# Cross-attention and a routed mixture of experts: the first five shared-expert steps run inside attention's last five, with the last tiles' routing behind them

## The chip, the cores and the metric

One core of one Trainium2 chip. The metric is the device time of one execution in microseconds (us), the slowest core's; here there is only one. Engines: TensorE (PE) multiplies matrices, VectorE (DVE), ScalarE (ACT) and GpSimd (POOL) work elementwise, SyncE (SP) issues DMAs. Each takes its instructions in the order of its own list and waits on semaphores.

## The reference

x is 4096 rows of 256 (4 batches of 1024), the context 4 x 64 rows of 192. Cut to what matters:

```python
x = x + attention(layernorm(x), ctx, Wq, Wk, Wv, Wo, bo)      # 16 heads of 64, 64 keys
xf = layernorm(x)                                              # rows for the experts
scores = softmax(xf @ gate_w.T); idx = top_k(scores + gate_b, 2)
expert(x) = silu((x @ w1 + b1) * (x @ w3 + b3)) @ w2 + b2      # 256 -> 352 -> 256
out = x + sum of the two chosen experts, weighted by their scores (8 experts) + shared expert
```

## The kernel before

The 4096 rows are 32 tiles of 128 (NT = 32). Weights are split into a high part in a rounded format and a low part, the rest; each product is three matmuls (high by high, high by low, low by high). The kernel has three stages.

**Preparation** (up to about 100 us) folds Wq with the keys and Wo with the values.

**Attention** is a software pipeline of steps s (lines 329 to 1407). In step s each engine works on several tiles: on TensorE (`tile_step`, L1329) scores of tile s-1, gate product of s-6 (L1360), transposes of the probabilities of s-3 (L1376), output product of s-4, and the transposes of the normalized xn2 of s-5 (L1404). These and the gate product share PSUM bank 0, so the transposes of tile t wait until the gate logits of t-1 are copied (`lg_ok`, L1398). On VectorE: maxima, sums, the low part pTl, x2 (L1083) with its statistics, and the logits copy (L1030). On GpSimd: reciprocal roots of the variance (L610 to L614, L605 on) and the scaling of the probabilities. On ScalarE: exponentials, xn2 (L766), pTh (L783) and xn2T (L759). Steps 33 to 37 have no scores left: the pipeline runs empty. In them ScalarE and VectorE also begin to split the experts' weights (`high13`, L882; `low13`, L1150). `begin_step` of each engine is what it does in a step besides `tile_step`.

**Routing** is done in groups of eight tiles. The three first groups (GROUPS) are routed in six small stages (`route`, L975) in steps of attention; the last eight tiles (REST) after it (`rest`, L1216). The routed rows are put in order by expert: GpSimd scatters a record of each row and choice to a table in DRAM (`scatter_record`, L665, three in flight, 64 in all, one tile of two per step from step 20 on), SyncE then loads 71 slices of it (L543), and GpSimd gathers the rows (`gather`, L714).

**Shared and routed steps** (`unit_step` of each engine: L906, L1164, L1409) are one pipeline over 103 tiles: 20 shared ones, 71 routed ones, 12 shared. In step s: the input of tile s is split (uxTh on ScalarE, L939; uxTl on VectorE, L1177), TensorE multiplies tile s-1 by w1 and w3 ("UV", 12 matmuls of 352 columns, L1464), VectorE adds the bias and multiplies (uv L1195, hid L1198), ScalarE applies SiLU to tile s-2 (L949), TensorE transposes hid of s-3 (L1456), ScalarE and VectorE split that (hTh L944, hTl L1182), and TensorE makes the output product of s-4 (L1440). The first twenty steps also carry the splitting of the other weights (`high2`, `low2`, `high13`, `low13`).

The order is written by hand for each engine. VectorE's, between attention and the common loop, is the one that the change rewrites: rest(0), step 0, rest(1), rest(2), step 1, rest(3), rest(4), step 2, rest(5), step 3, unit arithmetic, step 4, more unit arithmetic (L1221 to L1256). Tiles, DRAM scratch and buffers share SBUF over time: a region is given to later buffers when the work that used it is over, which the waits on `O_ok`, `lg_ok` and the DMA semaphores guard.

Of the kernel before, what the change touches and what calls it, by code (L numbers as in the profile page):

```python
# [13 lines left out]
P = 128  # L14
# [12 lines left out]
def xattn_moe(nc, x, ctx, Wq, Wk, Wv, Wo, bo, gate_w, gate_b, w1, b1, w3, b3, w2, b2,  # L27
# [23 lines left out]
    RING = 8  # L51
# [28 lines left out]
    with stack:  # L80
# [67 lines left out]

        xin = sb("xin", [P, 2, D], F32, att)
# [7 lines left out]

        pre = ExitStack()
        raw = ExitStack()
        wv_raw = sb("wv_raw", [P, 2, INNER], F32, raw)  # L160
        wo_raw = sb("wo_raw", [P, NJ, D], F32, raw)
        raw.close()
        wvl = sb("wvl", [P, 2, INNER], F32R, pre)
# [6 lines left out]

        xres = sb("xres", [P, 2, D], F32, att)
        xn2T = sb("xn2T", [P, 2, D], F32, att)
# [3 lines left out]
        x2 = sb("x2", [P, 2, D], F32, att)  # L176
        xn2 = sb("xn2", [P, 2, D], F32, att)
# [14 lines left out]
        gv = sb("gv", [P, 6, 8], F32, att)  # L192
# [32 lines left out]
        b13 = sb("b13", [P, E, 2 * H], F32)  # L225
# [6 lines left out]
        uv = sb("uv", [P, 2, H], F32)  # L232
        logits = sb("logits", [P, NT, E], F32)
# [7 lines left out]
        unit_no = sb("unit_no", [P, NU], F32)  # L241

# [142 lines left out]
        FILL = 5  # L385
        
# [59 lines left out]
        def _(sp):  # L446
# [51 lines left out]
            def load_w13(e):  # L498
                sp.wait_ge(O_ok, TPB if e < EARLY13 else 2 * TPB)
                sp.dma_start(w13_raw[:, e, :, 0:H], w1[e, :, :].rearrange("(k p) h -> p k h", p=P)).then_inc(raw13_in[e], 16)  # L500
                sp.dma_start(w13_raw[:, e, :, H:2 * H], w3[e, :, :].rearrange("(k p) h -> p k h", p=P)).then_inc(raw13_in[e], 16)
# [7 lines left out]
            def begin_step(s, par):  # L509
                tile_step(s, par)  # L510
                if s in (13, 14, 15, 16, 17):
                    load_w13(s - 13)
                if s in (21, 22, 23):
                    load_w13(s - 16)
                if 24 <= s < 24 + EARLY2:
                    load_w2(s - 24)
                if s in (31, 32):
                    load_w2(s - 25)
                if 24 <= s < 24 + RING:
                    for half in xn2T_out:  # L520
                        sp.wait_ge(half, 16 * RING // 2)
                    shared_x(s - 24)
# [22 lines left out]
            for t in range(RING, NA):  # L545
                shared_x(t)
# [30 lines left out]
        def _(pool):  # L577
# [93 lines left out]
            def begin_step(s, par):  # L671
# [22 lines left out]


            for half in xn2_out + x2_out:
                pool.wait_ge(half, before(NT))
            pool.wait_ge(O_ok, NT)
            pool.wait_ge(lg_ok, NT)
            pool.memset(hid[:, :, H:H3], 0.0).then_inc(hid_one, 1)  # L700
            pool.wait_ge(hid_one, 1)
            pool.memset(hid[:, :, H:H + 1], 1.0).then_inc(hid_one, 1)
# [24 lines left out]

            ahead = RING - 2
# [15 lines left out]
        def _(act):  # L744
# [118 lines left out]
            def begin_step(s, par):  # L863
# [4 lines left out]
                tile_step(s, par)  # L868
                if 33 <= s < 33 + EARLY13:
# [26 lines left out]
            act.wait_ge(zero_ok, 1)  # L896
            steps(NT, 1, 6, begin_step, begun=0)

            act.wait_ge(rt_sub, len(GROUPS) + 1)
            act.activation(rest_score[:, :, :], rest_marked[:, 0, :, :], ACT.Exp).then_inc(rt_exp, 1)  # L900

# [4 lines left out]
            def unit_step(s, m, routed=None):  # L906
# [4 lines left out]
                if has(t, NALL):  # L911
# [10 lines left out]
                    elif t < R0:  # L922
                        wait(act, Y_ok, t + 1)
                        wait(act, shared_row_out[y], 16 * (t // YRING))
# [32 lines left out]
            act.wait_ge(hid_one, 2)  # L957
            act.wait_ge(zero_out, 16 * (NB // QUAD + 3))
            unit_steps(act, unit_step)
# [3 lines left out]
        def _(dve):  # L963
# [196 lines left out]

            dve.wait_ge(small_in, 80)
            steps(NT, 2, 6, begin_step, begun=0)

            def unit_step(s, m, routed=None):  # L1164
# [19 lines left out]
                if has(t, NALL):  # L1184
                    p = (m + 1) % 2
                    if is_routed(t, routed):
                        e = dve.value_load(expert_of[0:1, bass.ds(t - R0, 1)], min_val=0, max_val=E - 1)
                        if isinstance(t, int) and t == R0:
                            dve.wait_ge(b13_in, 32 * E)
                        bias = b13[:, bass.ds(e, 1), :].rearrange("p e (a h) -> p (e a) h", a=2)  # L1190
# [20 lines left out]

            dve.wait_ge(lg_ok, NT)
# [32 lines left out]
            unit_step(4, 4)  # L1245
# [258 lines left out]
```

## Time and profile before

| | us |
|---|---|
| median of 3 runs | 722.57 (722.37 to 724.9) |
| the profiled execution | 728.77 |
| its span | 727.0 |
| TensorE busy | 671.5 (92%) |
| VectorE busy | 537.7 (74%) |
| GpSimd busy | 429.1 (59%) |
| ScalarE busy | 400.9 (55%) |

The span goes from the first to the last instruction of the profiled execution; 1.8 us of its time lie around it. Stages in it: preparation to about 100, attention to 337, shared steps of tiles 0 to 19 to 413, routed steps to about 665, the last shared ones and the sums to the end. Times below are microseconds from the start of the span. A view in order of time gives the start, the duration (overlapping a little with the next one's where an engine is pipelined), the line, the tiles and, in brackets, how long the engine was idle before and what ended it.

### The profile page before, as it was taken

What the parts mean: (1) busy time and instruction counts of PE and PEld (TensorE: products, weight loads), DVE (VectorE), ACT (ScalarE), POOL (GpSimd) and SP (SyncE); (2) the same over time, 40 slices, a digit from 0 to 9 for tenths busy, and PEclk for the clock granted to TensorE, in tenths of its full rate; (3) what the DMA queues carried; (4) which work ended last, traced back from release to release, by engine and by line L of the source; (5) the groups of instructions that cost most, each with busy time, mean ns of one, the idle gap of its engine ahead of it and who ended that gap; (6) DMA issues with size and microseconds to landing.
All of it is one profiled execution on the core that took longest, in us unless ns stands there. A gap on an engine that the chain in (4) does not pass through costs nothing.

```text
span 727.0 us, 16811 instructions
## 1 busy us (share of the span) xinstructions
PE 671.5 (92%) x4606; PEld 627.8 (86%) x4607; DVE 537.7 (74%) x1106; ACT 400.9 (55%) x1308; POOL 429.1 (59%) x514
## 2 busy tenths in 40 slices
PE   7997789999999989985699999999999999999976
PEld 6785679998888879874699999999999999999975
DVE  5964788888978878766989866666666666666796
ACT  4984677877767666664564444444444444444432
POOL 4552565454468677665346337677777777775291
PEclk8998999999999999996999999999999999999999
DMA  8201223336526875754851335554444444455694
GB/s 247 78 15 65 66 73 94 104 110 193 161 80 116 187 138 130 111 133 90 154 85 44 79 49 75 75 74 72 72 73 72 72 72 72 72 102 97 150 407 187
DMA packets 77045, 79.03 MB, mean 109 GB/s; under 512 B 21738, under 2 KB 70228, under 8 KB 76980
## 3 DMA queue, kind: packets, MB, share of 16 engines
q1 hardware_dynamic: 56932, 53.66, 29.3%
q0 software_dynamic: 15760, 18.96, 16.2%
q10 hardware_dynamic: 4288, 5.64, 2.4%
q8 instruction: 29, 0.48, 0.3%
q14 instruction: 36, 0.29, 0.2%
HBM read 47.22 MB, written 31.01 MB: 108 GB/s over the span
## 4 chain that ended last, share of the span: by engine, by line
PE 32%; issue 22%; POOL 13%; DMA 11%; SPq 9%; DVE 7%; ACT 5%; POOLq 0%; ACTq 0%; DVEq 0%
PE ps L1269 26%; DMA slots_scratch<-record,slot 8%; POOL xrow L718 6%; SPq L542 5%; SPq L543 4%; PE ps L1376 3%; POOL acc_scratch L725 2%; POOL slots_scratch L668 2%; DMA xin<-in_x 1%; PE ps L1360 1%; ACT prob L791 1%; DVE AU L1121 1%; DMA wk_raw<-in_L_xattn_Wk 1%; PE ps L1345 1%; ACT AU L803 1%
## 5 line engine op out<-in xcount | busy, mean ns | idle before, releaser
L725 POOL DMA_INDIRECT acc_scratch<-yrow,slots x71 | 112.7, 1587 | 70.2 <-ACT yrow L920 56.3
L920 ACT ACTIVATE yrow<-ps,slots 128x256 f32<-128x256 f32 x71 | 33.7, 474 | 147.7 <-PE ps L1269 147.7
L1269 PE MATMUL ps<-AU,pTh 128*128 128x256 f32 x512 | 101.3, 290 | 0.0
L1195 DVE TENSOR_TENSOR uv<-ps,b 128x704 f32<-128x704 f32 x71 | 63.3, 892 | 47.8 <-PE ps L1269 47.8
L1269 PE MATMUL ps<-w13h,uxTh 128*128 x284 | 97.8, 344 | 0.0
L1269 PE MATMUL ps<-AU,xTh 128*128 128x512 f32 x256 | 97.4, 425 | 0.0
L668 POOL DMA_INDIRECT slots_scratch<-record,slot x64 | 66.1, 1033 | 45.8 <-DMA slots_scratch<-record,slot 33.6
L1269 PE MATMUL ps<-w13h,uxTl 128*128 x284 | 91.6, 322 | 0.0
L1269 PE MATMUL ps<-w13l,uxTh 128*128 x284 | 91.3, 322 | 0.0
L718 POOL DMA_INDIRECT xrow<-xn_scratch,slots x71 | 69.8, 983 | 27.2 <-issue 19.8
L791 ACT ACTIVATE prob<-ps,nmax 128x64 f32<-128x64 f32 x256 | 76.3, 337 | 14.4 <-DVE nmax L1048 14.3
L1269 PEld LDWEIGHTS ps<-AU,pTh 128*128 128x128 f32 x512 | 82.3, 191 | 0.0
L621 POOL TENSOR_TENSOR prob<-prob,hinv 128x1024 f32<-128x1024 f32 x32 | 60.9, 1904 | 25.0 <-DVE hinv L1026 24.8
L1269 PE MATMUL ps<-AU,pTl 128*128 128x256 f32 x256 | 72.8, 284 | 0.0
L1269 PE MATMUL ps<-w2h,hTh 128*128 x213 | 63.2, 297 | 0.0
L1269 PE MATMUL ps<-w2l,hTh 128*128 x213 | 60.3, 283 | 0.0
L1269 PE MATMUL ps<-w2h,hTl 128*128 x213 | 60.0, 282 | 0.0
L1198 DVE TENSOR_TENSOR hid<-uv 128x352 f32<-128x352 f32 x103 | 56.9, 552 | 3.5
L791 ACT ACTIVATION_READ_ACCUMULATOR prob<-ps,nmax 128x1 f32 x256 | 59.2, 231 | 0.0
L1177 DVE TENSOR_TENSOR uxTl<-ps,uxTh 128x256 fp32r<-128x256 f32 x71 | 30.2, 425 | 38.4 <-ACT uxTh L939 37.9
L1269 PEld LDWEIGHTS ps<-AU,xTh 128*128 128x128 f32 x256 | 50.1, 196 | 9.0
L1182 DVE TENSOR_TENSOR hTl<-ps,hTh 128x384 fp32r<-128x384 f32 x103 | 57.3, 556 | 0.4 <-ACT hTh L944 0.4
(241 smaller groups left out, 2000.9 us busy)
## 6 DMA issues: line engine op xcount, KB each, us to landing
sums<-acc_scratch SPq DMA_DIRECT2D x16, 512.0 KB, 11.3
w_raw<-in_L_ffn_w SPq DMA_DIRECT2D x16, 352.0 KB, 4.1
xin<-in_x SPq DMA_DIRECT2D x32, 128.0 KB, 2.5
xres<-in_x SPq DMA_DIRECT2D x32, 128.0 KB, 3.0
acc_scratch<-x SPq DMA_DIRECT2D x32, 128.0 KB, 2.3
xn_scratch<-xn SPq DMA_DIRECT2D x32, 128.0 KB, 2.6
xn2T_scratch<-xn2T SPq DMA_DIRECT2D x32, 128.0 KB, 3.7
xrow<-xn2T_scratch SPq DMA_DIRECT2D x32, 128.0 KB, 5.0
```

The source lines that it names most:

```text
L542: row = sp.value_load(unit_row[0:1, u:u + 1], min_val=0, max_val=(BLOCKS - 1) * P)
L621: pool.tensor_tensor(heads, heads, hinv[:, p, :].unsqueeze(2).to_broadcast([P, HEADS, NK]), ALU.mult).then_inc(norm_ok, 1)
L668: pool.indirect_dma_start(slots_dram, bass.IndirectOffsetOnAxis(ap=slot[:, k, t:t + 1], axis=0), record[:, t, k, :], None).then_inc(scat_o ...
L718: pool.indirect_dma_start(xrow[:, m, :], None, xn2_dram, bass.IndirectOffsetOnAxis(ap=slots[:, u, 0:1], axis=0)).then_inc(gather_in[m], 16)
L725: pool.indirect_dma_start(acc_dram[u % 2], bass.IndirectOffsetOnAxis(ap=slots[:, u, 0:1], axis=0), yrow[:, m % YRING, :], None, compute_op ...
L791: act.activation(prob[:, p, h * NK:(h + 1) * NK], ps[:, s_bank(p) + h // 8, h % 8 * NK:(h % 8 + 1) * NK], ACT.Exp, bias=nmax[:, p, h - HS: ...
L920: act.activation(yrow[:, y, :], ps[:, 6 + m % 2, 0:D], ACT.Copy, scale=slots[:, bass.ds(u, 1), 1].bitcast(F32)).then_inc(y_ok, 1)
L1177: dve.tensor_tensor(uxTl[:, p, :], xT, f32(uxTh[:, p, :]), ALU.subtract).then_inc(uxTl_ok, 1)
L1182: dve.tensor_tensor(hTl[:, :], ps[:, 5, 0:H3], f32(hTh[:, :]), ALU.subtract).then_inc(hTl_ok, 1)
L1195: dve.tensor_tensor(uv[:, :, :], ps[:, 1 + 2 * p:3 + 2 * p, 0:H], bias, ALU.add).then_inc(bias_ok, 1)
L1198: dve.tensor_tensor(hid[:, p, 0:H], uv[:, 0, :], uv[:, 1, :], ALU.mult).then_inc(z_ok, 1)
L1269: last = pe.matmul(out, stationary(k, a), moving(k, b), start=(k == 0 and i == 0), stop=(k == n - 1 and i == len(PARTS) - 1 and not more))
```

## The change

`DRAIN` is NT + 1 = 33. In attention's steps 33 to 37 each engine now also runs shared step s - 33 behind its `tile_step`. Shared steps 5 to 9 then stand between the routing stages of the last eight tiles, on VectorE in the pattern that steps 0 to 4 had. Two low13 and one low2 more fall in these steps. The waits that guarded the shared steps move: GpSimd's memsets of hid go to step 33, its wait for the stores of x2 and xn2 behind the scatters, ScalarE's wait for the zeroed rows to its first shared output, and ScalarE waits for all stores of attention before the last tiles' exponential. The two biases of the eight experts are loaded whole, 128 rows of 11,264 bytes each, in place of sixteen loads with rows of 1,408 bytes. Four loads of xrow go ahead of them. Loads of w13 for experts 5 to 7 are spread over steps 20 to 25, those of w2 start two steps later. The four buffers xres, x2, xn2 and xn2T move down in SBUF, so that the buffers of the shared steps lie over ones that are dead in step 33.

```diff
+        xres = sb("xres", [P, 2, D], F32, att)
+        x2 = sb("x2", [P, 2, D], F32, att)
+        xn2 = sb("xn2", [P, 2, D], F32, att)
+        xn2T = sb("xn2T", [P, 2, D], F32, att)
...
-        b13 = sb("b13", [P, E, 2 * H], F32)
+        b13 = sb("b13", [P, 2, E, H], F32)
+        DRAIN = NT + 1
@@ SyncE, begin_step @@
-                if s in (13, 14, 15, 16, 17):
-                    load_w13(s - 13)
-                if s in (21, 22, 23):
-                    load_w13(s - 16)
-                if 24 <= s < 24 + EARLY2:
-                    load_w2(s - 24)
-                if s in (31, 32):
-                    load_w2(s - 25)
+                if 13 <= s < 13 + EARLY13:
+                    load_w13(s - 13, 0)
+                    load_w13(s - 13, 1)
+                if 20 <= s < 20 + 2 * (E - EARLY13):
+                    load_w13((s - 20) // 2 + EARLY13, s % 2)
+                if 26 <= s < 26 + EARLY2:
+                    load_w2(s - 26)
+                if s in (32, 33):
+                    load_w2(s - 26)
@@ SyncE, behind attention @@
-            for e in range(E):
-                for i, b in enumerate((b1, b3)):
-                    sp.dma_start(b13[:, e, i * H:(i + 1) * H],
-                                 b[e, :].rearrange("(a h) -> a h", a=1).to_broadcast([P, H])).then_inc(b13_in, 16)
+            for t in range(RING, RING + 4):
+                shared_x(t)
+            for i, b in enumerate((b1, b3)):
+                sp.dma_start(b13[:, i, :, :].rearrange("p e h -> p (e h)"),
+                             b.rearrange("(a e) h -> a (e h)", a=1).to_broadcast([P, E * H])).then_inc(b13_in, 16)
-            for t in range(RING, NA):
+            for t in range(RING + 4, NA):
                 shared_x(t)
@@ GpSimd, begin_step (and gone behind attention) @@
+                if s == DRAIN:
+                    pool.wait_ge(S_ok, NT)
+                    pool.memset(hid[:, :, H:H3], 0.0).then_inc(hid_one, 1)
+                    pool.wait_ge(hid_one, 1)
+                    pool.memset(hid[:, :, H:H + 1], 1.0).then_inc(hid_one, 1)
@@ ScalarE, begin_step @@
                 tile_step(s, par)
+                if s >= DRAIN:
+                    unit_step(s - DRAIN, s - DRAIN)
@@ ScalarE, unit_step @@
-                if isinstance(s, int) and 1 <= s < 1 + E // 2:
-                    high2(2 * s - 2)
-                    high2(2 * s - 1)
-                if isinstance(s, int) and 5 <= s < 5 + E - EARLY13:
-                    high13(s - 5 + EARLY13)
+                if isinstance(s, int) and 5 <= s < 5 + E:
+                    high2(s - 5)
+                if isinstance(s, int) and 5 + E <= s < 5 + E + E - EARLY13:
+                    high13(s - 5 - E + EARLY13)
@@ ScalarE, behind attention @@
+            for half in xn2_out + x2_out + xn2T_out:
+                act.wait_ge(half, before(NT))
             act.wait_ge(rt_sub, len(GROUPS) + 1)
             act.activation(rest_score[:, :, :], rest_marked[:, 0, :, :], ACT.Exp).then_inc(rt_exp, 1)
-            unit_steps(act, unit_step)
+            unit_steps(act, unit_step, begun=NT + 6 - DRAIN)
@@ VectorE, begin_step: behind tile_step and route, ahead of low13 @@
+                if s >= DRAIN:
+                    unit_step(s - DRAIN, s - DRAIN)
                 if s >= 35:
                     low13(s - 35)
@@ VectorE, unit_step @@
-                if isinstance(s, int) and 5 <= s < 5 + E:
-                    low2(s - 5)
-                if isinstance(s, int) and 5 + E <= s < 5 + E + E - 3:
-                    low13(s - 5 - E + 3)
+                if isinstance(s, int) and 6 <= s < 8:
+                    low13(s - 3)
+                if isinstance(s, int) and 8 <= s < 8 + E:
+                    low2(s - 8)
+                if isinstance(s, int) and 8 + E <= s < 8 + E + E - EARLY13:
+                    low13(s - 8 - E + EARLY13)
@@ VectorE, behind attention @@
             rest(0)
-            dve.wait_ge(hid_one, 2)
-            unit_step(0, 0)
+            unit_step(5, 5)
             rest(1)
             rest(2)
-            unit_step(1, 1)
+            unit_step(6, 6)
             rest(3)
             rest(4)
-            unit_step(2, 2)
+            unit_step(7, 7)
             dve.wait_ge(rank_ok, len(GROUPS) + 1)
             rest(5)
-            unit_step(3, 3)
+            unit_step(8, 0)
...
-            unit_step(4, 4)
+            unit_step(9, 1)
...
-            unit_steps(dve, unit_step, begun=5)
+            unit_steps(dve, unit_step, begun=10)
@@ TensorE @@
+            def begin_step(s, par):
+                tile_step(s, par)
+                if s == DRAIN:
+                    pe.wait_ge(exp_ok, NT)
+                    pe.wait_ge(sw_lo, 2)
+                if s >= DRAIN:
+                    unit_step(s - DRAIN, s - DRAIN)
+            steps(NT, 0, 6, begin_step)
-            for s in range(3):
+            for s in range(NT + 6 - DRAIN, 8):
                 unit_step(s, s)
             pe.wait_ge(chosen_ok, len(GROUPS) + 1)
+            pe.wait_ge(shared_row_ok, 4)
             ranks(7, rest_chosen, NREST).then_inc(rank_ok, 1)
-            unit_steps(pe, unit_step, begun=3)
+            unit_steps(pe, unit_step, begun=8)
```

## Rows read from the trace of the kernel before

**Rows 1.** the page: span, all engines

```profile
span 727.0 us, 16811 instructions
```

**Rows 2.** stretches: us, busy per engine (instructions), granted clock, DMA share, GB/s

```profile
330.00:335.00 5.00, 1.17 (x5) 0.78 (x5) 3.76 (x8) 2.76 (x5) 4.43 (x4) 0.59 0.16 53
355.00:360.00 5.00, 3.60 (x24) 3.31 (x24) 4.72 (x11) 2.56 (x7) 2.33 (x3) 1.00 0.79 122
413.55:680.00 266.45, 266.34 (x1921) 261.07 (x1921) 174.66 (x297) 112.39 (x297) 176.22 (x137) 1.00 0.46 76
```

**Rows 3.** who waited for whom, TensorE, 311.7 to 390: us in total, times, longest

```profile
PE ps L1269 <- DVE hTl L1182: 4.8, 3, 1.9
```

**Rows 4.** stretch from step 34 to shared tile 10, columns of rows 2

```profile
319.70:377.70 58.00, 41.78 (x282) 38.94 (x282) 45.47 (x109) 33.24 (x67) 27.99 (x33) 0.88 0.57 108
```

**Rows 5.** order of time, VectorE, one shared step: start, us, what, count, idle before

```profile
377.70 0.42 DVE L1177 TENSOR_TENSOR uxTl<-xrow,uxTh 128x256 fp32r<-128x256 f32 x1
378.04 0.55 DVE L1182 TENSOR_TENSOR hTl<-ps,hTh 128x384 fp32r<-128x384 f32 x1
378.94 0.89 DVE L1195 TENSOR_TENSOR uv<-ps,bs 128x704 f32<-128x704 f32 x1 [0.36 <-PE ps L1269]
...
380.31 0.95 DVE L1159 TENSOR_TENSOR w2l<-w_raw,w2h 128x768 fp32r<-128x768 f32 x1
381.18 0.41 DVE L1177 TENSOR_TENSOR uxTl<-xrow,uxTh 128x256 fp32r<-128x256 f32 x1
```

**Rows 6.** order of time, VectorE: attention's last steps, two low13 steps

```profile
324.59 0.17 DVE L1030 COPY logits<-ps 128x8 f32<-128x8 f32 x1
...
328.29 0.42 DVE L1083 TENSOR_TENSOR x<-ps,xres 128x256 f32<-128x256 f32 x1 [2.74 <-PE ps L1269]
...
330.47 1.69 DVE L1153 TENSOR_TENSOR w13l<-w_raw,w13h 128x704 fp32r<-128x704 f32 x2
332.07 0.16 DVE L1030 COPY logits<-ps 128x8 f32<-128x8 f32 x1
...
335.58 0.17 DVE L1030 COPY logits<-ps 128x8 f32<-128x8 f32 x1 [1.75 <-PE ps L1360]
...
337.30 0.06 DVE L1214 MEMSET rest_chosen<- 128x4 uint32 x1
...
392.13 0.41 DVE L1177 TENSOR_TENSOR uxTl<-xrow,uxTh 128x256 fp32r<-128x256 f32 x1
...
395.89 0.42 DVE L1177 TENSOR_TENSOR uxTl<-xrow,uxTh 128x256 fp32r<-128x256 f32 x1
```

**Rows 7.** order of time, TensorE: last transpose of xn2, an UV block, tile 20

```profile
332.89 0.69 PE L1404 MATMUL ps<-ident,xn 128*128 128x128 f32 x2 [3.33 <-ACT xn L766]
...
347.50 0.43 PE L1269 MATMUL ps<-ws13h,uxTh 128*128 128x352 f32 x1 [0.21 <-DVE uxTl L1177]
...
349.36 0.32 PE L1269 MATMUL ps<-ws13l,uxTh 128*128 128x352 f32 x1
...
412.66 0.38 PE L1448 MATMUL ps<-ident,xrow 128*128 128x128 f32 x2
```

**Rows 8.** order of time: ScalarE's table load; POOL's memset, last scatter, first gather

```profile
343.82 1.28 ACT L949 ACT_TABLE_LOAD   x1
...
335.89 0.15 POOL L700 MEMSET hid<- 128x64 f32 x1 [0.66 <-DVE logits L1030]
...
400.41 0.96 POOL L668 DMA_INDIRECT slots_scratch<-record,slot  x1 [1.43 <-DMA slots_scratch<-record,slot]
406.21 1.16 POOL L718 DMA_INDIRECT xrow<-xn_scratch,slots  x1 [4.84 <-DMA slots<-slots_scratch]
```

**Rows 9.** stretch 337.3 to tile 5, columns of rows 2; two VectorE waits

```profile
337.30:360.74 23.44, 16.54 (x96) 15.19 (x96) 19.61 (x58) 14.55 (x27) 9.55 (x10) 0.85 0.88 164
...
338.86 0.43 DVE L1177 TENSOR_TENSOR uxTl<-xrow,uxTh 128x256 fp32r<-128x256 f32 x1 [0.98 <-ACT uxTh L939]
...
343.33 0.89 DVE L1195 TENSOR_TENSOR uv<-ps,bs 128x704 f32<-128x704 f32 x1 [1.35 <-PE ps L1269]
```

More of the change, by code:

```diff
@@ L147, in xattn_moe @@
         Uh, Ul = (AU[:, :, i, :].rearrange("p b (j d) -> p b j d", j=NJ) for i in (2, 3))
+        pre = ExitStack()
+        raw = ExitStack()
+        wv_raw = sb("wv_raw", [P, 2, INNER], F32, raw)
+        raw.close()
+        wvl = sb("wvl", [P, 2, INNER], F32R, pre)
+        pre.close()
+        xres = sb("xres", [P, 2, D], F32, att)
+        x2 = sb("x2", [P, 2, D], F32, att)
+        xn2 = sb("xn2", [P, 2, D], F32, att)
+        xn2T = sb("xn2T", [P, 2, D], F32, att)
         xin = sb("xin", [P, 2, D], F32, att)
@@ L169, in xattn_moe @@
         pre.close()
-        xres = sb("xres", [P, 2, D], F32, att)
-        xn2T = sb("xn2T", [P, 2, D], F32, att)
         prob = sb("prob", [P, 2, HK], F32, att)
@@ L175, in xattn_moe @@
         pTl = sb("pTl", [P, 2, HK], F32R, att)
-        x2 = sb("x2", [P, 2, D], F32, att)
-        xn2 = sb("xn2", [P, 2, D], F32, att)
         st2 = sb("st2", [P, 2, 6], F32, att)
@@ L191, in xattn_moe @@
         rank = sb("rank", [P, 8 + 1, E], F32, att)
-        gv = sb("gv", [P, 6, 8], F32, att)
         att.close()
@@ L241, in xattn_moe @@
         unit_no = sb("unit_no", [P, NU], F32)
+        gv = sb("gv", [P, 6, 8], F32)
         ps = stack.enter_context(nc.psum_tensor("ps", [P, 8, BANK], F32))
@@ L496, in _, with load_w13 @@
             sp.wait_ge(pre_dve, NPRE)
-            def load_w13(e):
+            def load_w13(e, half):
                 sp.wait_ge(O_ok, TPB if e < EARLY13 else 2 * TPB)
-                sp.dma_start(w13_raw[:, e, :, 0:H], w1[e, :, :].rearrange("(k p) h -> p k h", p=P)).then_inc(raw13_in[e], 16)
-                sp.dma_start(w13_raw[:, e, :, H:2 * H], w3[e, :, :].rearrange("(k p) h -> p k h", p=P)).then_inc(raw13_in[e], 16)
+                sp.dma_start(w13_raw[:, e, :, half * H:(half + 1) * H],
+                             (w1, w3)[half][e, :, :].rearrange("(k p) h -> p k h", p=P)).then_inc(raw13_in[e], 16)
             def load_w2(e):
@@ L693, in _ @@
             steps(NT, 1, 5, begin_step, begun=1)
[L696 to L702, printed above, removed]
             pool.wait_ge(slot_ok, len(GROUPS))
@@ L726, in scatter_add @@
                                         yrow[:, m % YRING, :], None, compute_op=ALU.add).then_inc(y_out[u % 2], 16)
+            for half in xn2_out + x2_out:
+                pool.wait_ge(half, before(NT))
             ahead = RING - 2
@@ L894, in high2 @@
                 act.activation(flat[0], flat[1], ACT.Copy).then_inc(w2_hi, 1)
[L896 to L900, printed above, removed]
             def shared_z(t):
@@ L923, in unit_step @@
                         wait(act, Y_ok, t + 1)
+                        if t == 0:
+                            act.wait_ge(zero_out, 16 * (NB // QUAD + 3))
                         wait(act, shared_row_out[y], 16 * (t // YRING))
@@ L949, in unit_step @@
                     act.activation(hid[:, p, 0:H], hid[:, p, 0:H], ACT.Silu).then_inc(h_ok, 1)
-                if isinstance(s, int) and 1 <= s < 1 + E // 2:
-                    high2(2 * s - 2)
-                    high2(2 * s - 1)
-                if isinstance(s, int) and 5 <= s < 5 + E - EARLY13:
-                    high13(s - 5 + EARLY13)
-            act.wait_ge(lg_ok, NT)
-            act.wait_ge(hid_one, 2)
-            act.wait_ge(zero_out, 16 * (NB // QUAD + 3))
-            unit_steps(act, unit_step)
+                if isinstance(s, int) and 5 <= s < 5 + E:
+                    high2(s - 5)
+                if isinstance(s, int) and 5 + E <= s < 5 + E + E - EARLY13:
+                    high13(s - 5 - E + EARLY13)
+            act.wait_ge(zero_ok, 1)
+            steps(NT, 1, 6, begin_step, begun=0)
+            act.wait_ge(lg_ok, NT)
+            for half in xn2_out + x2_out + xn2T_out:
+                act.wait_ge(half, before(NT))
+            act.wait_ge(rt_sub, len(GROUPS) + 1)
+            act.activation(rest_score[:, :, :], rest_marked[:, 0, :, :], ACT.Exp).then_inc(rt_exp, 1)
+            unit_steps(act, unit_step, begun=NT + 6 - DRAIN)
         @block.vector
@@ L1159, in low2 @@
                 dve.tensor_tensor(flat[0], flat[1], f32(flat[2]), ALU.subtract).then_inc(w_lo, 1)
-            dve.wait_ge(small_in, 80)
-            steps(NT, 2, 6, begin_step, begun=0)
             def unit_step(s, m, routed=None):
@@ L1188, in unit_step @@
                         if isinstance(t, int) and t == R0:
-                            dve.wait_ge(b13_in, 32 * E)
-                        bias = b13[:, bass.ds(e, 1), :].rearrange("p e (a h) -> p (e a) h", a=2)
+                            dve.wait_ge(b13_in, 32)
+                        bias = b13[:, :, bass.ds(e, 1), :].rearrange("p a e h -> p a (e h)")
                     else:
@@ L1210, in unit_step @@
                                       ALU.add).then_inc(out_ok, 1)
+            dve.wait_ge(small_in, 80)
+            steps(NT, 2, 6, begin_step, begun=0)
             dve.wait_ge(lg_ok, NT)
@@ L1405, in tile_step @@
                     last.then_inc(T2_ok, 1)
-            steps(NT, 0, 6, tile_step)
             def unit_step(s, m, routed=None):
@@ L1452, in unit_step @@
                     p = (m + 1) % 2
+                    if isinstance(t, int) and t == 0:
+                        pe.wait_ge(hid_one, 2)
                     wait(pe, h_ok, t + 1)
```

4 lines of the change are left out of this document (removed).

## The prediction

> **What bounds the kernel now.** I read four views. First the page: the span is 727.0 us [rows 1]; the profiled execution lasted 728.77 us, 6.2 above the median of the runs shown (722.57), so I work out a difference against the profiled execution and take it from the median. Second, the stretches: from 413.55 to 680 TensorE is busy 266.34 of 266.45 us [rows 2], so a microsecond won before tile 20 is a microsecond of the whole, as long as tile 20's gathered row is there in time. Third, the seam between attention and the shared steps: the granted clock is 0.59 in 330 to 335 (0.5 is 1.2 GHz, 1.0 is 2.4 GHz), and in 355 to 360 TensorE works 3.60 of 5 us while VectorE works 4.72 [rows 2]. Fourth, who waits for whom: behind the seam TensorE's largest sum is 4.8 us in three waits, for VectorE's hTl [rows 3]. So the seam has two limits: a chain of latencies up to 337, then VectorE, with routing, unit arithmetic and weight splitting in one queue, until about 409.
>
> That decides what to ask. The change does not take work from VectorE. It moves five shared steps (their part on VectorE) from the VectorE-bound stretch to the latency-bound one. It wins what VectorE's idle time there really absorbs. Between 319.7 and the uxTl of shared tile 10 at 377.70 VectorE is busy 45.47 of 58.00 us [rows 4]: 12.5 us is the most that could be won.
>
> **Prices of a shared step on VectorE** [rows 5]: uxTl to hTl 0.35, hTl 0.54 (0.90 less the 0.36 idle), uv and hid 1.37 (378.94 to 380.31), low2 0.87 (380.31 to 381.18). A whole step is 2.25 without low2. A low13 is 1.69 for its two halves, of which I take 1.67, the next start overlapping a little [rows 6]. On TensorE an UV block is 2.0 us (347.50 to 349.36 and its last 0.3) [rows 7].
>
> **The tail with the steps in it.** VectorE's and ScalarE's queues are in order, so each inserted step stands before the next attention step. Times of before are in [rows 6].
> 1. Step 33: POOL's two memsets of hid now stand ahead of the tail's normalizations. They were the 0.15 at 335.89 [rows 8] and a shorter one; with issue gaps 0.4. It is ahead of xn2, pTh and pTl, so all behind it is +0.4.
> 2. Step 34: shared step 1 (uxTl, uv, hid: 1.7) stands before the logits copy of 324.59, which goes to 326.8. TensorE's rank sum and the output product of the last tile wait for that copy. x2 of 328.29 goes to 330.5 (+2.2).
> 3. Step 35: low13 of 330.47 is first pushed by 2.2 and then by step 2 (1.7), and starts at 334.4; the logits copy of 332.07 comes at 336.1 (+4.0). The transpose of xn2 on TensorE (332.89) overwrites the same PSUM bank and waits for it: 336.3.
> 4. Step 36: behind the transpose TensorE has the hid transposes (0.4) and UV of tile 2 (2.0), to 339.2. ScalarE has hTh, SiLU and a split of weights (1.5) ahead of the last xn2T, which is done at 339.9 and its gate product at 340.5. VectorE adds uv from 339.3, hid and low13 to 342.3, so the last logits copy goes from 335.58 to 342.4 (+6.8).
> 5. Step 37: TensorE then has the first shared output product (about 1.2), hid transposes and UV of tile 3, to 344.1. VectorE: uv, hid, low13 to 347.3. The memset that opens the routing of the last tiles goes from 337.30 to 347.3: **+10.0 us**.
>
> **After the tail.** Before, VectorE goes from 337.30 to the uxTl of tile 5 at 360.74 in 23.44 us, 19.61 of them busy [rows 9]. Inside are five uxTl, four uv with hid, two hTl (8.31) and waits of 0.98 and 1.35 [rows 9]; routing and unit arithmetic are the rest, 12.8 (between 11.3, busy time alone, and 15.1, with all waits). After, the same 12.8 stand between steps 5 to 9: five whole steps (11.25), two low13 (3.34), two low2 (1.74) and one wait for ScalarE, whose exponential of the last tiles comes before uxTh of tile 5 (1.2). Sum 30.3, so the uxTl of tile 10 is at 347.3 + 30.3 = 377.6, against 377.70 now. From there to the first gathered transposes at 412.66 [rows 7] two steps with low13 (3.76 apart, 392.13 to 395.89) become two with low2 (about 3.4) [rows 5, 6]: 0.7 less. **Sum: -0.1 - 0.7 = -0.8 us.** What VectorE no longer idles after the seam, it idles before: it waits for the last output product, for the hid transposes, and for UV of tiles 2 and 3.
>
> **Edits costed at nothing, with their cover.** Two bias loads for sixteen: SP issues fewer, and VectorE first needs them at routed tile 20, over 60 us later. Four xrow loads move ahead of them; each has more than four shared steps. The w2 loads come two steps later but high2 starts four shared steps later. ScalarE's new wait for the last xn2T store (landing some 4 us after 339.9) ends at 344, before VectorE's subtraction at 347.9. TensorE's wait for four shared rows stands behind step 7, which needs row 3 anyway. The other buffer layout moves no instruction.
>
> **The activation table.** SiLU now comes once in the tail, then Exp for the last tiles, then SiLU again: two more table loads. The row has 1.28 us for one [rows 8]. I add nothing: SiLU of tile 0 is needed only behind the transpose at 336.3; ScalarE waits from 344.6 to 347.9 in any case; and SiLU of tile 3 is needed at 351.6, behind TensorE's output product, with ScalarE free from 349.5.
> The Trainium skill ("ScalarE: Activation LUTs", "What ACT_TABLE_LOAD costs") adds 1380 ns of drain to the 1283 of the load, 2.66 us per switch. The trace agrees on the load and shows no drain as a row of its own. With the whole 2.66 SiLU of tile 3 would end a microsecond later and my sum would be -0.2 instead of -0.8.
>
> **Rivals.**
> A, faster: the idle time does absorb the steps. For it: 12.5 us idle, and the inserted work is only 8.31. If all of it fits, the time is 722.6 - 8.3 = 714.3; if the chains 2 and 4 hide half of it, 718. Against: the inserted uv waits for UV blocks that TensorE issues behind attention's own work, and the gate logits share one bank. Chance 0.28.
> B, slower: the bias loads hold up the slot scatters. Now thirty scatters run after the tail, 2.2 us apart, to 400.41; the first gather is at 406.21, and about 3 us later the row is there, some 3.4 before TensorE transposes it at 412.66 [rows 7, 8]. The pitch is set by landing and three in flight, not by POOL's 0.96. From 335.5 they would end at 399 and the chain stays hidden. But the same 2.9 MB of biases now move in packets of 11,264 bytes for 1,408. If scatters stand still for the 10 us in which the biases move, less the three or four that pass now, the chain ends 6 to 8 us later; beyond about 4 it decides the time. Then +4 to +5: 727. Chance 0.12.
> The Trainium skill ("DMA: Bandwidth & Descriptors", "Queues, rings and completion order") says that a DMA engine takes turns between queues a packet at a time, which speaks for B; no row before shows a bias packet of the new size.
> C, the clock: in my walk TensorE idles 3.0 us at 333 to 336. Before, the clock fell to half behind the gap from 329.5 on [rows 2]. If it falls at step 36, UV of tile 2 takes 3.6 for 2.0, and the tail ends 1.4 to 3.5 later: 723.2 to 725.3. Chance 0.10; it mostly stays within my bound for no change.
>
> **The numbers.** Half a per cent (3.6 us) is about what a measurement of this kernel can tell from none. Forecast: 722.6 - 0.8 = 721.8, chance 0.50; its own range, from hops mis-set by a few tenths each and routing between its two ends, is 719 to 724.5. Faster by over 0.5%: most of A and a little of the forecast, 0.28. Slower by over 0.5%: B, and the worst of C and of the forecast, 0.19. Within: 0.53. The range for 8 in 10 takes in half of A's way and B: 715.5 to 727.5.
>
> **What would show it.** Right: the memset of rest_chosen near 347, ten microseconds later than now; uxTl of tile 10 within a microsecond of 377.7; VectorE's waits for TensorE grown between 327 and 345; two more table loads. Wrong in favour of A: that memset at 341 or earlier. Wrong in favour of B: TensorE waiting at the transposes of xrow for a gather. C: a granted clock near half between 336 and 345.

## The result and the profile after

The changed kernel takes 728.62 us (median of 20 executions, 724.22 to 739.07), the kernel before on the same chips 725.19 (722.37 to 729.03, 20). The ratio is 1.0043 [1.0024, 1.0062]: slower by 0.4%. That is inside the half per cent that I called no change, but it has the other sign than my 0.8 us and lies above my range. Part of that is the base: the prediction put the kernel before at 722.57, the median of three executions, and here it takes 725.19. As a difference the change costs 3.4 us, and my range went to 4.9 above the kernel before. Two later comparisons gave 0.9989 [0.9954, 1.0024] and 1.0052 [1.0025, 1.0079]. Single executions differ by 7 us (before) and 15 us (changed), so I read the cause from stretches of the traces, where the three traces of the changed kernel agree within 0.1 us. Ratios leave out executions over 1.5% above the fastest of their kernel, and three of the traces below (after_again, a_fill, a_fillwarm) are of such executions.

The page of after, for [rows 1]:

```profile
span 730.8 us, 16802 instructions
```

The profiled execution took 732.56 us. Its span is 3.8 us longer than before. To place them I count from x2 of tile 29 (317.12 before, 316.60 after), the last one ahead of the inserted steps, to the uxTl of shared tile 10 (377.70 and 381.52): **60.58 us before, 64.92 after**. From there to the first transposes of gathered rows it is 34.96 and 34.14, and behind them 314.34 and 315.14. So the seam costs 4.3 us, 0.8 come back behind it, and 0.8 are lost at the end.

The seam as one stretch, first before, then after: length, busy time (and instructions) of PE, PEld, DVE, ACT and POOL, granted clock, DMA share, GB/s.

```profile
317.12:377.70 60.58, 43.89 (x299) 40.87 (x298) 47.77 (x118) 33.62 (x68) 30.16 (x36) 0.89 0.57 111
```

```profile
316.60:381.52 64.92, 50.13 (x302) 48.25 (x301) 47.91 (x120) 30.72 (x62) 34.08 (x40) 0.82 0.42 109
```

VectorE's busy time is the same (47.77, 47.91), as the prediction said. TensorE does about as many instructions in 6.2 us more: its granted clock is 0.82 instead of 0.89. With 1.0 for 2.4 GHz and 0.5 for 1.2, that is 23.4 us at half clock (64.92 x 0.18 x 2) against 13.3. Stretches of the seam after, same columns, show where, beside those of before in [rows 2]:

```profile
328.00:330.00 2.00, 2.00 (x11) 2.00 (x11) 0.00 (x0) 1.29 (x2) 0.74 (x1) 0.50 0.01 1
335.00:340.00 5.00, 2.89 (x14) 2.92 (x15) 2.90 (x6) 2.16 (x5) 3.78 (x5) 0.78 0.12 29
345.00:350.00 5.00, 3.65 (x25) 3.30 (x24) 3.67 (x8) 1.80 (x3) 2.31 (x3) 1.00 0.61 63
350.00:355.00 5.00, 2.96 (x13) 2.96 (x14) 3.71 (x11) 4.53 (x10) 1.30 (x2) 0.64 1.01 346
355.00:360.00 5.00, 5.00 (x26) 5.00 (x26) 2.82 (x8) 2.06 (x6) 2.28 (x3) 0.67 0.97 325
360.00:365.00 5.00, 2.45 (x23) 2.07 (x22) 4.73 (x14) 1.75 (x4) 1.11 (x2) 1.00 0.39 132
365.00:370.00 5.00, 5.00 (x26) 4.89 (x26) 4.54 (x12) 2.25 (x5) 2.47 (x3) 0.66 0.34 56
375.00:380.00 5.00, 3.72 (x16) 3.72 (x17) 4.86 (x9) 1.39 (x4) 2.97 (x3) 0.53 0.33 26
```

A stretch in which TensorE has gaps (2.45 of 5 us busy in 360 to 365) is followed by one at a clock of 0.66, in which it is busy all 5 us. Before there was one long fall, from 330 to 344.5. For most of it TensorE had almost nothing to do (1.17 of 5 us at 0.59, [rows 2]); the one long piece of work in it was the first UV block, at its end. Two stretches of before:

```profile
335.00:340.00 5.00, 1.11 (x5) 1.04 (x6) 3.26 (x11) 2.74 (x7) 3.04 (x6) 0.50 0.27 64
340.00:345.00 5.00, 5.00 (x20) 5.00 (x19) 3.38 (x11) 2.13 (x3) 1.70 (x2) 0.54 1.00 160
```

Now there are five shorter falls, near 327, 338, 351, 365 and 375, and they lie on work that VectorE waits for. VectorE in order of time, for [rows 6] and [rows 9] (start, us, line, what, count; in brackets idle before and its releaser):

```profile
331.37 0.42 DVE L1089 TENSOR_TENSOR x<-ps,xres 128x256 f32<-128x256 f32 x1 [4.24 <-PE ps L1277]
...
336.85 0.16 DVE L1036 COPY logits<-ps 128x8 f32<-128x8 f32 x1
...
341.35 0.89 DVE L1200 TENSOR_TENSOR uv<-ps,bs 128x704 f32<-128x704 f32 x1 [2.38 <-PE ps L1277]
...
344.34 0.15 DVE L1036 COPY logits<-ps 128x8 f32<-128x8 f32 x1
...
348.20 0.06 DVE L1223 MEMSET rest_chosen<- 128x4 uint32 x1
...
351.05 0.42 DVE L1182 TENSOR_TENSOR uxTl<-xrow,uxTh 128x256 fp32r<-128x256 f32 x1 [2.26 <-ACT uxTh L942]
...
358.49 0.89 DVE L1200 TENSOR_TENSOR uv<-ps,bs 128x704 f32<-128x704 f32 x1 [2.04 <-PE ps L1277]
...
381.52 0.41 DVE L1182 TENSOR_TENSOR uxTl<-xrow,uxTh 128x256 fp32r<-128x256 f32 x1
```

The 2.26 before 351.05 lead to ScalarE, where one row stands out:

```profile
348.89 1.28 ACT L964 ACT_TABLE_LOAD   x1 [3.20 <-DVE rest_marked L1000]
350.18 0.26 ACT L964 ACTIVATE rest_score<-rest_marked 128x64 f32<-128x64 f32 x1
```

ScalarE idles 3.20 us for VectorE's subtraction and only then loads the exponential's table. uxTh of tile 5 stands behind it, uxTl and hTl behind that, and TensorE's next product waits for hTl. TensorE after:

```profile
348.68 0.32 PE L1277 MATMUL ps<-ws13l,uxTh 128*128 128x352 f32 x1
352.04 0.58 PE L1277 MATMUL ps<-ws2h,hTh 128*128 128x256 f32 x1 [3.04 <-DVE hTl L1187]
352.42 0.42 PE L1277 MATMUL ps<-ws2h,hTl 128*128 128x256 f32 x1
```

Behind this gap the 256-column matmuls take 0.42 us; at full clock they take 0.28.

### The profile page after: what moved, and what is told of

Read it like the earlier page. It is cut to its first block, busy times and chain, and to the rows that moved or that the text cites. A ratio compares the mean times of both kernels' runs of the same rounds, so it can differ in the third digit from the quotient of the medians.

```text
span 730.8 us, 16802 instructions
## 1 busy us (share of the span) xinstructions
PE 678.6 (93%) x4606; PEld 635.8 (87%) x4607; DVE 536.9 (73%) x1106; ACT 403.6 (55%) x1310; POOL 429.2 (59%) x514
## 4 chain that ended last, share of the span: by engine, by line
PE 73%; DVE 11%; issue 5%; ACT 5%; POOL 3%; DMA 2%; SPq 0%; ACTq 0%; DVEq 0%; POOLq 0%
PE ps L1277 60%; PE ps L1464 4%; PE ps L1384 3%; PE ps L1454 2%; ACT prob L796 1%; DVE uv L1200 1%; DMA xin<-in_x 1%; PE ps L1368 1%; DMA wk_raw<-in_L_xattn_Wk 1%; DVE AU L1127 1%; DVE w13l L1161 1%; PE ps L1353 1%; POOL slots_scratch L675 1%; DVE hmax L1051 1%; DVE hTl L1187 1%
## 5 line engine op out<-in xcount | busy, mean ns | idle before, releaser
L728 POOL DMA_INDIRECT acc_scratch<-yrow,slots x71 | 112.1, 1580 | 76.3 <-ACT yrow L921 57.0
L796 ACT ACTIVATE prob<-ps,nmax 128x64 f32<-128x64 f32 x256 | 76.5, 338 | 13.4 <-DVE nmax L1054 13.4
L796 ACT ACTIVATION_READ_ACCUMULATOR prob<-ps,nmax 128x1 f32 x256 | 59.3, 232 | 0.0
```

The lines of the kernel that those rows point to most:

```text
L728: pool.indirect_dma_start(acc_dram[u % 2], bass.IndirectOffsetOnAxis(ap=slots[:, u, 0:1], axis=0), yrow[:, m % YRING, :], None, compute_op ...
L796: act.activation(prob[:, p, h * NK:(h + 1) * NK], ps[:, s_bank(p) + h // 8, h % 8 * NK:(h % 8 + 1) * NK], ACT.Exp, bias=nmax[:, p, h - HS: ...
```

## The experiments

**The theory**: the new order is as good as the old one for VectorE; what it loses is the clock (TensorE's work now lies in bursts with gaps between) and the table load that stands in the path. **Rivals**: the bias loads; the order itself; the scatters.

All marks count from x2 of tile 29, as above: "seam" to the uxTl of tile 10, "tile 20" to the first transposes of gathered rows. Before is 60.6 and 95.5, after 64.9 and 99.1. Ratios are against the kernel before on the same chip.

**1. The two causes, each and together.** Filler transposes go into a part of PSUM that nobody reads at that time, at the places where TensorE waits:

```diff
+            def warm(n, bank=0):
+                for _ in range(n):
+                    pe.transpose(ps[:, bank, 2 * P:3 * P], ident[:, :], ident[:, :])
@@ ranks of step 35 / last xn2 transposes of step 36 / head of unit_step / ahead of the ranks behind step 7 @@
+                        if s == 35: warm(18, 7)
+                    if s == 36: warm(24, 7)
+                    warm({6: 18, 7: 8, 8: 12, 9: 12, 10: 24, 11: 16}.get(s, 0))
+            warm(12)
```

> The changed kernel, with transposes of the identity added on TensorE in the seam's gaps (18 and 24 in steps 35 and 36, 6 to 24 ahead of shared steps 6 to 11), whose results nobody reads. Theory 1 (the granted clock: TensorE's work is spread thin over the seam and the clock falls to half five times, so that VectorE waits for UV blocks): the clock stays at 1.0 from 326 to 385, the gathered transposes of tile 20 come 2 to 3.5 us earlier than 415.66, and the time is 725 to 726.5. Theory 2 (the in-order queues of VectorE and ScalarE alone): the time stays at 728.6 or grows by what the transposes add.

The table is asked for before the wait, with an activation of one column into a buffer that is dead by then:

```diff
+            act.activation(eps[:, :], gateb_bc[:, 0:1], ACT.Exp)
             act.wait_ge(rt_sub, len(GROUPS) + 1)
             act.activation(rest_score[:, :, :], rest_marked[:, 0, :, :], ACT.Exp).then_inc(rt_exp, 1)
```

> The changed kernel, with one tiny exponential on ScalarE ahead of its wait for the last tiles' subtraction, so that the Exp table is loaded while ScalarE is idle. Theory 2 (ScalarE's table switch stands on the path: 1.28 us between the subtraction and uxTh of tile 5): VectorE's wait of 2.26 us at uxTl of tile 5 falls to about 1, time 727.3. Theory 1 (VectorE's later waits for TensorE at half clock take it back): 728 to 728.6.

Both edits, in two runs on two chips, each beside the changed kernel once more:

> The changed kernel with the added transposes and the early table load together. Theory 1 (clock): both causes of the gaps behind the tail are gone, so the stretch from x2 of tile 29 to uxTl of tile 10 is 60.5 to 61.5 us, as before, and the time is that of the kernel before within 0.2%. Theory 2 (in-order queues alone): the stretch shrinks by the 1.3 us of the table load alone, to 63.6.

> The changed kernel itself, for a comparison on one chip. Both theories: 0.2 to 0.6% above the kernel before. Its trace shows by how much one execution differs from another: by theory 1 the stretches at half clock may lie elsewhere, and the stretch from x2 of tile 29 to uxTl of tile 10 (60.6 us before, 64.9 in the first trace of the changed kernel) follows the time spent at half clock.

> a_both again, on the same chip as after3. If clock and table load are the cause, its median is 3 to 5 us below after3's and within 0.3% of before; if the cause lies elsewhere, it equals after3.

> The changed kernel again: 0.2 to 0.6% above before, the seam from x2 of tile 29 to uxTl of tile 10 at 64.9 us.

| | clock in seam | seam | tile 20 | ratio |
|---|---|---|---|---|
| changed (three traces) | 0.82 | 64.9, 64.9, 65.0 | 99.1, 99.0, 99.1 | 1.0043, 0.9989, 1.0052 |
| a_warm | 0.97 | 63.4 | 101.3 | 1.0016 [0.9978, 1.0055] |
| a_preload | 0.94 | 61.5 | 98.5 | 1.0058 [1.0021, 1.0094] |
| a_both | 1.00 | 59.1 | 93.3 | 1.0018 [0.9990, 1.0046] |
| a_both2 | 1.00 | 59.1 | 93.3 | 0.9988 [0.9956, 1.0021] |

Both edits take 5.8 us from the seam, 3.4 by the table alone and 1.6 by the filler alone. a_warm's 1.6 holds a stall that has nothing to do with its edit: 28.7 us behind the mark VectorE waits 1.99 us although TensorE has finished the product.

```profile
342.83 0.89 DVE L1200 TENSOR_TENSOR uv<-ps,bs 128x704 f32<-128x704 f32 x1 [1.99 <-remote]
```

The seams of a_preload, and then of a_both2:

```profile
313.18:374.66 61.48, 44.76 (x305) 42.03 (x303) 47.83 (x119) 30.72 (x63) 31.95 (x38) 0.94 0.48 116
```

```profile
311.98:371.06 59.08, 56.68 (x449) 54.52 (x447) 47.91 (x119) 30.74 (x63) 29.99 (x37) 1.00 0.51 123
```

VectorE is busy 47.91 us in a_both2 as in the changed kernel: only its waits went. In a_preload the load stands where ScalarE would idle anyway. ScalarE, then VectorE:

```profile
342.40 1.28 ACT L963 ACT_TABLE_LOAD   x1
343.69 0.20 ACT L963 ACTIVATE eps<-gateb_bc 128x1 f32<-128x1 f32 x1
345.44 0.26 ACT L965 ACTIVATE rest_score<-rest_marked 128x64 f32<-128x64 f32 x1 [1.55 <-DVE rest_marked L1001]
...
346.58 0.43 DVE L1183 TENSOR_TENSOR uxTl<-xrow,uxTh 128x256 fp32r<-128x256 f32 x1 [1.17 <-ACT uxTh L942]
```

VectorE's wait goes from 2.26 to 1.17, so 1.1 us is the direct price. The seam gained 3.4. Most of the rest is the clock: TensorE's gap at this place shrinks from 3.04 to 1.96 us, and behind it the clock stays up. TensorE, then a stretch:

```profile
347.57 0.38 PE L1278 MATMUL ps<-ws2h,hTh 128*128 128x256 f32 x1 [1.96 <-DVE hTl L1188]
347.79 0.28 PE L1278 MATMUL ps<-ws2h,hTl 128*128 128x256 f32 x1
```

```profile
350.00:355.00 5.00, 4.23 (x30) 3.94 (x30) 4.79 (x12) 3.14 (x9) 0.96 (x1) 1.00 1.02 316
```

Up to the memset of rest_chosen the two traces are alike (31.60 and 31.64 us behind the mark, both at a granted clock of 0.89); from it to the uxTl of tile 10 it is 33.32 us at 0.75 and 29.84 at 1.00. The half-clock time of the seam falls from 23.4 to 7.4 us. Filler on top of that gains ahead of the memset (29.43 in a_both) and next to nothing behind it (29.68); filler with the late load, in a_warm, leaves 31.64 us at 0.95 behind it. So of the 5.8 us the table's place accounts for 3.5 and the clock ahead of the memset for 2.2. With one table load moved, all three falls behind the memset are gone.

It is not that TensorE has less idle time in a_preload, nor is it the length of one gap alone. In the changed kernel the falls come in or just behind gaps of 1.92, 3.29, 3.04 and 3.00 us, and one comes behind two gaps of 1.50 and 1.06 with little work between them. In a_preload gaps of 2.63 and 2.69 us, at 369.32 and 375.60, are followed by 256-column matmuls of 0.28 us, that is by the full clock. What decides between them is not shown.

The time of the whole follows less well. a_both2 is 5.6 us under the changed kernel on its chip (724.70 and 730.31), but a_both's 1.0018 stands beside 0.9989 for the changed kernel on the other, where no gain shows; a_preload's gain shows in no ratio, and the changed kernel was not run beside it. So that the two causes make the seam longer is shown; that removing them makes the kernel faster was seen on one chip of two. Three reasons can be named. Most of the spread of single executions lies ahead of the mark, where none of these edits reaches: x2 of tile 29 comes at 311.16 in a_both and at 322.65 in a_fill. The four traces a_warm, a_preload, b_warm and b_bias, taken together while the kernel before took 732.8 us (726.5 and 725.7 in the next two groups), each have a stall of 2.4 to 4.1 us 93 to 98 us behind the mark, which the other traces with three scatters in flight don't have; it is most of what makes tile 20 late in a_warm (uxTl of tile 10 to tile 20: 37.9 instead of 34.1) and in a_preload (37.0), and what causes it is open. And part is given back at the end: behind tile 20's transposes the three traces of the changed kernel take 315.0 to 315.2 us, a_both 317.5, a_both2 317.8. Up to 275 us behind those transposes they agree within 0.2; then, where GpSimd adds up the results, TensorE waits once for 2.83 us in a_both2, where the changed kernel's longest wait is 2.07:

```profile
690.12 0.38 PE L1278 MATMUL ps<-ws2h,hTh 128*128 128x256 f32 x1 [2.83 <-DVE hTl L1188]
```

So about 2.5 of 5.8 us come back as a loss there. Why the last stage takes longer is open.

**2. Does the old order gain by the same filler?** The same transposes in the kernel before: 24 in step 36 and `{1: 30, 4: 8, 5: 14, 6: 14}` at the heads of shared steps.

> The kernel before, with the same kind of transposes in its own gaps (24 ahead of the last transpose of xn2, 30 ahead of the first UV block, 8 to 14 ahead of shared steps 4 to 6). Theory 1, clock: the one long stretch at half clock (330 to 344.5) goes, which was worth only VectorE's one wait of 1.35 us for the first UV block, so 724 against 725.2. Theory 2: no difference.

```profile
321.17:380.07 58.90, 51.11 (x387) 47.54 (x386) 47.32 (x118) 33.41 (x67) 28.82 (x34) 1.00 0.50 114
```

The clock is 1.00 and the seam 58.9 (60.6 without filler), ratio 0.9991 [0.9949, 1.0033]. At full clock both orders need 58.9 to 59.1 us. In the seam the order itself is neither better nor worse. To tile 20 it is 95.3 us in b_warm and 93.3 in a_both; 0.8 of that is the shorter stretch with low2 for low13, the rest is a last stretch of 36.4 us in b_warm's trace instead of 34.96, whose cause is open. At the clock that the chip grants without filler the old one pays 1.7 us and the new one 5.8, 1.1 of them the table directly.

**3. The bias loads alone.** In the kernel before:

```diff
-        b13 = sb("b13", [P, E, 2 * H], F32)
+        b13 = sb("b13", [P, 2, E, H], F32)
...
-            for e in range(E):
-                for i, b in enumerate((b1, b3)):
-                    sp.dma_start(b13[:, e, i * H:(i + 1) * H], ...)
+            for i, b in enumerate((b1, b3)):
+                sp.dma_start(b13[:, i, :, :].rearrange("p e h -> p (e h)"), ...)
```

> The kernel before with the biases in two loads and their new layout, nothing else of the change. The chain of slot scatters has some 3.4 us of slack before, so by both theories no difference (within 0.2%); the rival B of the prediction, large bias packets that hold up the scatters, would give 1 to 5 us more and TensorE waiting at the transposes of xrow.

The ratio is 0.9967 [0.9927, 1.0007], and the last scatter comes 79.96 us behind the mark instead of 83.29. The seam of this trace is 2.3 us longer (62.9 instead of 60.6) and tile 20 comes at 102.8, with stalls again of the open kind, so I take nothing finer from it. The chain of scatters itself repeats only roughly: its end lies at 80.6, 82.3 and 82.8 in the three traces of the changed kernel, at 81.4 and 78.5 in a_both and a_both2. GpSimd, its last scatter and first gather, for [rows 8]:

```profile
394.94 0.96 POOL L667 DMA_INDIRECT slots_scratch<-record,slot  x1 [0.30 <-issue]
400.34 1.43 POOL L717 DMA_INDIRECT xrow<-xn_scratch,slots  x1 [4.43 <-DMA slots<-slots_scratch]
```

Rival B does not hold here: with the larger packets the scatters end no later. In the changed kernel the gather for tile 20 starts at 404.25 and TensorE needs it at 415.66.

**4. Fill the gaps with VectorE's own work.** With the table loaded early, the first low13 goes into the wait for the last output product of attention, the second behind the uxTl of tile 3:

```diff
                     p = par
+                    if s == 35:
+                        low13(0)
                     wait(dve, O_ok, t + 1)
...
-                if s >= 35:
+                if s >= 37:
                     low13(s - 35)
...
+                if isinstance(s, int) and s == 3:
+                    low13(1)
```

> The changed kernel with the early table load, and with two of VectorE's low13 put where it idles: the first ahead of the last x2, the second behind uxTl of tile 3. What the prediction's walk says: the last two logits copies come 1.7 and about 3.2 us earlier, the memset of rest_chosen 16.9 us behind the last x2 becomes 13.5, and the stretch to uxTl of tile 10 is 58 to 59 us if the clock holds. Time 0.4 to 0.7% below the changed kernel's, about 0.2% below before. If only the clock mattered, it would be as the early table load alone (61.5).

> The same as a_fill with the added transposes of a_warm. Theory 1: the clock holds in every execution, stretch 57 to 58 us, time 0.3% below before, with a smaller spread than the kernels without added transposes. Rival: the transposes now stand in TensorE's way, since the gaps they were sized for are shorter, and the stretch is longer than a_fill's.

a_fill: seam 59.3, tile 20 at 96.7, ratio 1.0018 [0.9988, 1.0048]. a_fillwarm, with the filler transposes: 58.5, 96.4, 0.9980 [0.9945, 1.0015]. Against a_both (59.1, 93.3) the seam is not longer, yet tile 20 comes 3 us later. TensorE, then GpSimd, in a_fillwarm:

```profile
414.42 0.69 PE L1469 MATMUL ps<-ident,xrow 128*128 128x128 f32 x2 [3.58 <-DMA xrow<-xn_scratch,slots]
```

```profile
401.55 0.95 POOL L675 DMA_INDIRECT slots_scratch<-record,slot  x1 [2.42 <-DMA slots_scratch<-record,slot]
402.81 1.30 POOL L675 DMA_INDIRECT slots_scratch<-record,slot  x1 [0.30 <-issue]
411.19 1.00 POOL L721 DMA_INDIRECT xrow<-xn_scratch,slots  x1 [7.08 <-DMA slots<-slots_scratch]
```

The wait for the gathered row, which my rival B looked for, is here. The last scatter lies 84.7 us behind the mark, the gather 93.1. The seam is only 0.6 us shorter than in a_both; what differs is the chain, which ended at 81.4 and 78.5 there, with the gather at 89.4 and 86.0, and ends at 85.4 and 84.7 in a_fill and a_fillwarm. Why it ends later in the kernels with the moved low13 isn't shown.

**5. Are the biases part of that after all?** The two bias loads go behind the last shared row's load, with the filler transposes and without:

> a_fillwarm with the two bias loads issued behind the last xrow load of the shared stage instead of ahead of it. If the bias loads hold up the scatters (rival B of the prediction), the last scatter comes 3 to 6 us earlier than the 84.7 us behind x2 of tile 29, TensorE no longer waits for the first gathered row, and that comes at 92.5 to 93.5 instead of 96.35; time 0.3 to 0.6% below before. If not, nothing moves.

> The same without the added transposes: the last scatter as early as in a_late; the gathered transposes at 93 to 94 if the clock mostly holds, as in a_fill (7 us at half clock).

a_late: last scatter 84.0, tile 20 at 95.6 after a wait of 3.0; ratio 1.0045 [1.0013, 1.0076]. a_latecold: 84.7, 95.8, wait 0.85; 1.0026 [0.9994, 1.0057]. The biases' place moves the end of the scatters by 0.7 and 0.6 us, less than two traces of one kernel differ (2.8), where rival B asked for 3 to 6. The pair shows a second thing: the seams are 58.3 and 60.6, tile 20 comes at the same time. Where the scatter chain decides, a better clock in the seam is worth nothing.

**6. Six scatters in flight instead of three.** `FLIGHT = 6`, and to free semaphores the sums wait on the one of the raw weights, on counts behind its own. In a_fill, in a_fillwarm, and in b_warm:

> a_fill with six slot scatters in flight for three (and the semaphores of the last sums shared with those of the w13 loads, to free some). In a_fill and a_fillwarm TensorE waited 3.1 and 3.6 us at the first gathered transposes: with the seam shorter, the chain of scatters, three in flight, is the next limit. Theory: the last scatter comes earlier than 83 us behind x2 of tile 29 (from 85.4), TensorE's wait at the transposes of xrow goes, and they come 93.5 behind x2 of tile 29 instead of 96.7. Rival: the scatters' pitch is set by the DMA engines and not by the number in flight, and nothing changes.

> The same with the added transposes of a_warm: clock 1.0 over the seam, the gathered transposes 92.5 to 93.5 us behind x2 of tile 29 (95.5 in the kernel before), and a time 0.3 to 0.5% below before. If the seam isn't what decides, within 0.2% of before.

> The kernel before with the transposes of b_warm and six scatters in flight, nothing of the change: does the old order gain as much from the clock alone? By the prediction's count (the change moves VectorE's work and takes none away) the seam is 58.9 us to uxTl of tile 10, as with three in flight, and the gathered transposes come 94 us behind x2 of tile 29: 0.1 to 0.3% below before, and as fast as the changed kernel with both fixes (a_both). If the interleaving is worth something in itself, it is behind a_best by over 1 us in the seam.

The chain does get shorter: in a_flight the last scatter is at 74.2 us behind the mark (85.4 in a_fill), in a_best at 75.6 and in b_wf at 67.2. But the ratios are 1.0139 [1.0105, 1.0174], 1.0218 [1.0183, 1.0254] and 1.0083 [1.0049, 1.0117]; the seams are 65.8, 78.7 and 76.3, and tile 20 comes at 109.7, 115.7 and 112.0. A miss. The shared semaphore is hardly the reason: its new waits stand only at the sums at the end, and behind tile 20 these traces take 314.7 to 314.9 us, no more than the changed kernel. The loss lies in the seam and behind it, and not only in queues that wait for scatters: in a_best ScalarE idles 17.70 us ahead of one copy of an output row, and TensorE's filler transposes, which wait for nothing, start with gaps of up to 1.69 us that the trace counts as issue. What six scatters in flight take from them is not shown.

No version that I built is clearly faster than the kernel before.

## Why the prediction was wrong

**What bounds the kernel: right.** The seam in two limits, TensorE without idle time behind tile 20, VectorE's work moved and not removed: the rows of the five seams with 47.3 to 47.9 us of VectorE show it, and so do the equal 58.9 and 59.1 at full clock.

**The walk, step by step**, us relative to the mark where I compare differences:
- Step 1, GpSimd's memsets "+0.4": 0.41.
- Step 2, x2 of the last tile at 330.5: 331.37, with 0.5 less on the mark, so 1.4 late. VectorE waits 4.24 for the output product, at a clock of 0.50 from 328 on. With the clock held it is 13.27 us behind the mark; the walk had 13.4.
- Steps 3 and 4, logits copies at 336.1 and 342.4: 336.85 and 344.34.
- Step 5, the memset "+10.0 us" to 347.3: 348.20, relative to the mark +11.4. With filler the same distance is 29.43 us (a_both), where the walk had 30.2.
- Behind it I had 30.3 us to the uxTl of tile 10: 33.32. This is the largest miss. a_preload measures 29.84.
- The stretch to tile 20, -0.7: -0.8.

The sum to tile 20 is +3.5 where I had -0.8: 1.4 in the tail, 3.0 behind the memset, 0.1 less in the last stretch.

**The step that failed** is "The activation table. ... I add nothing". Its cover was named: "ScalarE waits from 344.6 to 347.9 in any case". ScalarE did wait, 3.20 us, but the load stands behind the wait, not in it (348.89). My 1.2 us for VectorE's wait is right only with the load moved ahead (1.17); it was 2.26. And with the load behind the wait the clock fell three times behind the memset, with it moved ahead not once, so that 1.1 us became 3.5. The Trainium skill ("ScalarE: Activation LUTs", "What ACT_TABLE_LOAD costs") has 1380 ns of drain beside the load; I would have been nearer with it, but for a reason that these traces don't show: the activation follows 0.01 us behind the load (348.89 + 1.28, then 350.18). The missing microsecond was the load's place.

**The clock (rival C) was the right rival at too small a size.** I let it fall once, at step 36, for 1.4 to 3.5 us of tail. It fell there (from 338 on, and VectorE waited 2.38 us for UV of tile 2) and one step earlier too, at the output product. Against the walk the tail lost 1.4, against the same tail at full clock 2.2. But I took the clock behind the memset for 1.00, as before in 355 to 360 [rows 2], and there it fell three times more. A walk that adds waits must ask at each new gap what TensorE does behind it.

**Rival A** was wrong in sign: the idle time absorbs no more than the walk said, and at full clock the seams of the two orders are equal. **Rival B** put the gather wait on the bias loads. Experiments 3 and 5 bear out neither part, though the wait itself is real and is the next limit. From the start of the gather to the transposes it takes 3.1 to 3.6 us where TensorE waits for it; in a_both and a_both2 it is 3.9 and 7.2, so about half a microsecond and 4 us of room are left. In a_fill, a_fillwarm, a_late and a_latecold it decides, at 95.6 to 96.7.

**The other edits costed at nothing**: the traces show no wait of theirs in the seam. The ratio, with an interval of 1.4 us either way, can't exclude some tenths.

## What to carry to other kernels

Work moved into a stretch of latencies must not only fit there: it also changes where TensorE's clock falls. Count the half-clock time of the stretch, before and after, from the granted clock, and see whose wait the slow work is; the lengths of the gaps alone did not tell it here. A table load is hidden only if the activation that asks for it stands ahead of the wait; one column is enough. And when a stretch gets shorter, look for the next chain at once: here, with seams of 58 to 61 us, the chain of 64 scatters set tile 20 at 95.6 to 96.7 us in four versions.

## What the runs showed that I had not expected

- The half clock is set off by a small difference: with a gap of 3.04 us and one of 1.96 at the same place, half-clock time in the seam was 23.4 and 7.4 us. Yet gaps of 2.63 and 2.69 us elsewhere set off no fall.
- With filler the granted clock is 1.00 over the whole seam; without it TensorE does 50.1 us of busy time in 64.9 at 0.82. Idle time on an engine that is not the bottleneck had a price here.
- After a wait of 3.0 and 3.6 us for the gathered row the next 50 us have a clock of 0.97 (a_late, a_fillwarm), and what follows comes 1.4 to 1.5 us later than behind tile 20 of a_both: such a wait costs more than its length.
- Six scatters in flight shortened their chain by 11 us (a_fill to a_flight) and made the kernel 0.8 to 2.2% slower.
- Single executions of one kernel on one chip spread by 5 us and more in both directions, while the seam in three traces of the changed kernel repeats within 0.1 us. For a change of half a per cent the stretch was the sharper measure. Not every mark is that firm: the end of the scatter chain moves by 2 to 3 us from trace to trace.
